# A sandwich layer on eight cores: the weight casts moved behind the first input loads, and a chunk's closing work moved into the next chunk's loop

## The reference, cut to what matters

```
def _L0_attn_ref(x, Wqkv, bqkv, Wout, bout):
    xc = x.reshape(N, Ls, Cc, Kk)                       # 32 blocks of 64
    qkv = jnp.einsum('nlck,cki->nlci', xc, Wqkv) + bqkv
    q, k, v = jnp.split(qkv, 3, axis=-1)
    scores = jnp.einsum('nlcd,nled->nldce', q, k) / Kk ** 0.5
    attn = jax.nn.softmax(scores, axis=-1)
    ctx = jnp.einsum('nldcm,nlcd->nldm', attn, v)
    ctx = ctx.transpose(0, 1, 3, 2)
    out = jnp.einsum('nlck,ko->nlco', ctx, Wout) + bout
    return out.reshape(N, Ls, Cc * Kk)

x = x + _layernorm(_L0_attn_ref(_layernorm(x), ...))
x = x + _layernorm((silu(xn @ w_gate.T) * (xn @ w_up.T)) @ w_down.T)   # xn = _layernorm(x)
```

## Time and profile before

| what | us |
|---|---|
| three runs | 6568.31, 6579.35, 6715.45 |
| median | 6579.35 |
| the profiled execution, whole time | 6572.25 |
| its span on the slowest core (core 3) | 6570.6 |
| spans of the other cores | 6551.8 to 6570.3 |
| busy on core 3: PE, DVE, ACT, POOL | 3205.5, 3231.0, 2051.9, 16.4 |

### The profile page before, as it was taken

One profiled execution on the slowest core, in us unless ns is written; L12 is line 12 of the kernel. 1 busy time (PEld: TensorE's weight loads), 2 busy tenths in 40 slices (PEclk: granted clock), 3 DMA queues, 4 the chain that ended last, 5 costly groups with the idle time before them and its releaser, 6 DMA issues.

```text
span 6570.6 us, 47652 instructions; the slowest of 8 cores (6551.8 to 6570.6 us)
## 1 busy us (share of the span) xinstructions
PE 3205.5 (49%) x15536; PEld 1485.4 (23%) x15536; DVE 3231.0 (49%) x3684; ACT 2051.9 (31%) x2953; POOL 16.4 (0%) x34
## 2 busy tenths in 40 slices
PE   0000010110048596850586867606767765089994
PEld 0000000000023233320232333203333322034441
DVE  0000008667757565747575657385756574721112
ACT  0000013444344444332443444324434433221210
POOL 0000000000000000000000000000000000000000
PEclk9999999655569797975797979757979887599997
DMA  9999970000023242321232322213323321144442
GB/s 113 111 111 110 111 81 0 7 7 0 7 74 122 64 136 80 112 65 38 86 116 71 122 93 100 65 38 100 103 87 106 103 87 64 35 144 141 154 141 87
DMA packets 177941, 556.83 MB, mean 85 GB/s; under 512 B 49568, under 2 KB 65952, under 8 KB 174496
## 3 DMA queue, kind: packets, MB, share of 16 engines
q1 hardware_dynamic: 171840, 442.60, 20.6%
q0 software_dynamic: 5856, 111.18, 15.0%
HBM read 639.73 MB, written 125.83 MB: 117 GB/s over the span
## 4 chain that ended last, share of the span: by engine, by line
DVE 30%; PE 24%; another core or an unknown queue 14%; ACT 12%; issue 12%; DMA 6%; DVEq 1%; ACTq 0%; SPq 0%
PE dps L415 10%; DVE es_sb L321 8%; DVE ctx_sb L330 6%; PE gps L353 6%; PE ups L363 6%; DVE zs_sb L752 4%; DVE zs_sb L746 4%; DMA wd_sb<-wdc 3%; ACT kd_sb L262 2%; DMA x2s_sb<-x2h 2%; ACT e_sb L376 1%; ACT m_sb L379 1%; ACT e_sb L373 1%; PE mps L189 1%
## 5 line engine op out<-in xcount | busy, mean ns | idle before, releaser
L353 PE MATMUL gps<-xn_sb,wg_sb 128*128 128x512 bf16 x4096 | 1002.9, 401 | 182.5 <-DVE gated_sb L388 167.5
L415 PE MATMUL dps<-gated_sb,wd_sb 128*128 128x512 bf16 x4096 | 920.1, 383 | 81.5 <-DMA wd_sb<-wdc 48.6
L363 PE MATMUL ups<-xn_sb,wu_sb 128*128 128x512 bf16 x4096 | 925.8, 379 | 0.0
L774 ACT ACTIVATE es_sb<-es_sb 128x4096 bf16<-128x4096 bf16 x256 | 922.0, 3602 | 11.4 <-DVE es_sb L737 11.4
L249 PE MATMUL mps<-xn_sb,wqkv_sb 128*128 128x128 bf16 x512 | 72.4, 302 | 1483.9 <-DVE xn_sb L804 1432.5
L763 ACT ACTIVATE rz_sb<-zf_sb 128x128 bf16<-128x128 bf16 x256 | 79.2, 309 | 2052.1 <-DVE zf_sb L756 2052.1
L202 DVE TENSOR_SCALAR st_sb<-mps 1x128 f32<-1x128 f32 x48 | 13.4, 279 | 1432.9 <-PE mps L189 1432.9
L383 DVE TENSOR_TENSOR t_sb<-m_sb,gps 128x512 bf16<-128x512 bf16 x256 | 175.9, 687 | 889.6 <-ACT m_sb L379 868.6
L321 DVE TENSOR_TENSOR es_sb<-es_sb,u_sb 128x4096 bf16<-128x4096 bf16 x256 | 586.7, 2292 | 27.7 <-DVE u_sb L312 1.4
L737 DVE TENSOR_TENSOR es_sb<-q_sb,kd_sb 128x4096 bf16<-128x4096 bf16 x256 | 586.0, 2290 | 24.4 <-DVE ctx_sb L330 0.9
L353 PEld LDWEIGHTS gps<-xn_sb,wg_sb 128*128 128x128 bf16 x4096 | 413.6, 102 | 741.4 <-issue 322.3
(11 more groups left out here) (85 smaller groups left out, 2033.0 us busy)
## 6 DMA issues: line engine op xcount, KB each, us to landing
wg_sb<-wgc SPq DMA_DIRECT2D x256, 512.0 KB, 3.5
wu_sb<-wuc SPq DMA_DIRECT2D x256, 512.0 KB, 3.3
wd_sb<-wdc SPq DMA_DIRECT2D x256, 512.0 KB, 3.4
wgc<-wgH POOLq DMA_DIRECT2D x4, 8192.0 KB, 434.4
wuc<-wuH POOLq DMA_DIRECT2D x4, 8192.0 KB, 509.6
wdc<-wdH POOLq DMA_DIRECT2D x4, 8192.0 KB, 585.3
yT<-outs_sb SPq DMA_DIRECT2D x64, 256.0 KB, 2.9
xb_sb<-xH POOLq DMA_DIRECT2D x16, 512.0 KB, 8.8
```

What stands on the lines that cost most here:

```text
L353: return tn.matmul(out=gps[pb].ap(), lhsT=wg_sb[pb].ap()[:, ft * 128:(ft + 1) * 128], rhs=xn2_sb.ap()[:, ft * W:(ft + 1) * W], start=(ft = ...
L363: return tn.matmul(out=ups[pb].ap(), lhsT=wu_sb[pb].ap()[:, ft * 128:(ft + 1) * 128], rhs=xn2_sb.ap()[:, ft * W:(ft + 1) * W], start=(ft = ...
L415: return tn.matmul(out=dps[pb].ap(), lhsT=wd_sb[wb].ap()[:, sh * 128:(sh + 1) * 128], rhs=gated_sb.ap()[:, ht * W:(ht + 1) * W], start=(ht ...
L774: ta = plan.op("A", lambda a, buf=buf: a.activation(out=buf.ap(), in_=buf.ap(), func=AF.Exp, scale=0.125), deps=[last[f"s_{c}_{j}"]], inc="A")
```

## The change

It has three parts. First, the casts are no longer issued ahead of everything: two are issued at the head of each pass of the loop until the list is empty, gate and up first, down last. Second, the closing work of a chunk is cut in two functions. `post_a` (the `wout` matmuls and the evictions to `ao_sb`) stays at the head of the next pass. `post_b` (all the rest, with `emit_xn2prep`, the spill and `dma_xb(c + 2)`) is called at j = 3 of the next chunk's attention loop, ahead of the pull. Third, there is no pull at j = 0, 1 and 2; at j = 3 there is a `pull(8)`, and from j = 4 on `pull(2)` as before. The number of atoms in a pass is the same. For c = -1 and c = 16, which have no attention, `post_a` and `post_b` follow each other directly.

```
-    for s in range(4):
-        for name_, dst_, src_ in (("g", wgc, wgT), ("u", wuc, wuT),
-                                  ("d", wdc, wdT)):
-            def fcache(g, dst_=dst_, src_=src_, s=s):
-                return g.dma_start(out=dst_[s * 2048:(s + 1) * 2048, :],
-                                   in_=src_[s * 2048:(s + 1) * 2048, :])
-            last[f"wc{name_}{s}"] = plan.op("G", fcache, inc=f"Dwc{name_}{s}")
+    _castd = {"g": (wgc, wgT), "u": (wuc, wuT), "d": (wdc, wdT)}
+
+    def emit_cast(name_, s):
+        dst_, src_ = _castd[name_]
+        def fcache(g, dst_=dst_, src_=src_, s=s):
+            return g.dma_start(out=dst_[s * 2048:(s + 1) * 2048, :],
+                               in_=src_[s * 2048:(s + 1) * 2048, :])
+        last[f"wc{name_}{s}"] = plan.op("G", fcache, inc=f"Dwc{name_}{s}")
+
+    CASTQ = [("g", 0), ("u", 0), ("g", 1), ("u", 1), ("g", 2), ("u", 2),
+             ("g", 3), ("u", 3), ("d", 0), ("d", 1), ("d", 2), ("d", 3)]
...
+        for _ in range(2):
+            if CASTQ:
+                emit_cast(*CASTQ.pop(0))
+
+        if 0 <= c < NC:
+            post_a()
+
         def pull(k):
...
-        if 0 <= c - 1 < NC:
-            cp = c - 1
-            ctx_tok = last[f"ctx_{cp}"]
...
+        def post_a():
+            if 0 <= c - 1 < NC:
+                cp = c - 1
+                ctx_tok = last[f"ctx_{cp}"]
...
+                last["ao"] = te
+                last[f"ctxdone_{cp}"] = te
+
+        def post_b():
+            if 0 <= c - 1 < NC:
+                cp = c - 1
+                tsq = plan.op("A", lambda a: a.activation(
+                    out=sq_sb.ap(), in_=ao_sb.ap(), func=AF.Square),
+                    deps=[last["ao"]] + dep("sq_free"), inc="A")
...
+            if 0 <= c - 1 < NC and (c - 1) % CPW == CPW - 1:
+                emit_xn2prep((c - 1) // CPW)
+
+            if 2 <= c + 2 < NC:
+                dma_xb(c + 2)
...
-                pull(2)
+                if j == 3:
+                    post_b()
+                if j >= 3:
+                    pull(8 if j == 3 else 2)
                 if j >= 1:
                     emit_uP(c, j - 1)
                 if j < NJ:
                     emit_exp(j)
+        else:
+            post_a()
+            post_b()
```

More of the change, by code:

```diff
@@ L615, in pull @@
                     emit_fin(a[1], a[2])
-        if 0 <= c - 1 < NC:
-            cp = c - 1
-            ctx_tok = last[f"ctx_{cp}"]
[L620 to L709, removed]
+        def post_a():
+            if 0 <= c - 1 < NC:
+                cp = c - 1
+                ctx_tok = last[f"ctx_{cp}"]
+                te = None
+                for grp in range(4):
+                    b = next_mbank()
+                    bank_dep = dep(f"pm{b}", "wout") + [ctx_tok]
+                    tk = None
+                    fst = True
+                    for i in range(4):
+                        mp = grp * 4 + i
+                        for par in (0, 1):
+                            m = 2 * mp + par
+                            def fn(tn, m=m, i=i, b=b, par=par):
+                                return tn.matmul(
+                                    out=mps[b].ap()[64 * par:64 * par + 64,
+                                                    i * T:(i + 1) * T],
+                                    lhsT=wout_sb.ap()[:, 64 * par:64 * par + 64],
+                                    rhs=ctx_sb.ap()[:, m * T:(m + 1) * T],
+                                    start=True, stop=True,
+                                    tile_position=(0, 64 * par),
+                                    skip_group_check=True)
+                            tk = plan.op("T", fn, deps=bank_dep if fst else (),
+                                         inc="T" if (i == 3 and par == 1) else None)
+                            fst = False
+                    def fe(a, grp=grp, b=b):
+                        return a.activation(
+                            out=ao_sb.ap()[:, grp * 4 * T:(grp + 1) * 4 * T],
+                            in_=mps[b].ap()[:, 0:4 * T], func=AF.Identity,
+                            bias=bo_sb.ap()[:, 0:1])
+                    d = [tk] + (dep("ao_free") if grp == 0 else [])
+                    te = plan.op("A", fe, deps=d, inc="A")
+                    last[f"pm{b}"] = te
+                last["ao"] = te
+                last[f"ctxdone_{cp}"] = te
```

49 lines of the change are left out of this document (added).

## The result

The changed kernel takes 6249.05 us as the median of ten runs (6127.99 to 6320.15), the kernel before in its own ten 6647.94 (6568.31 to 6790.34). The comparison gives a ratio of 0.9324, 95% interval 0.931 to 0.9339: faster by 6.8%. In both kernels some executions (five of ten before, six of ten after) are 2 to 3% longer, with a lower granted clock on the cores of one die, so the ratio and the times of runs from here on are of the others, 6128 to 6137 for the changed kernel.

What follows compares the result with a forecast made beforehand. The first 937 us were taken as bound by a queue order, input behind twelve casts. Sum: 6572.25 - 912 (front) + 68 (late load) + 4 (closing work) + 387 (piece of eight) = 6119, range 6035 to 6195.

Steps and rivals of the forecast that it cites:

- The front: Start of the kernel: with the casts behind the input, the first xb_sb lands at 25, not 936.8; gain 912.
- Chunk 2's late load: Chunk 1's first score product waits for chunk 2's input, queued behind two loads and four casts; cost 68.
- The third rival: Engines overlap the eight atoms at j = 3 as before, leaving only the queue's gain: 5732; chance 0.06.
- the fourth: Chunk 2's load is not held up because the DMA engines interleave it with the casts: 6051; chance 0.06.
- The closing work: Moved to j = 3, its waits come back there and it hides nothing: cost 4 over chunks 1 to 3.
- The boundary: Between chunks, L800 to first score product: falls to 30.3 from 47.3, or from 62.0 in chunks 4, 8, 12.
- The piece of eight: Eight atoms at j = 3, uncovered by attention, cost their full time: 129 a window, 387 over three windows.
- kind of chunk: Place in a four-chunk window; first to fifth score product: first 131.1, third 117.7, fourth 121.5; second: 78.6 to first down.
- the later loads have room: Input loads after chunk 2's land before they are wanted: chunk 3's near 491 for 572, chunk 4's near 646 for 805.
- the correction from the profiled execution to the median: Last step of the sum: profiled execution, 6572.25, is 0.1% under the median of three runs, so no correction.
- The first rival: Six casts from chunk 1 on starve beside DVE, delaying inputs of chunks 4, 5, 6 (+236, +309, +180): 6844; chance 0.04.
- The second rival: TensorE stays near its lower clock in the bursts, so 96 atoms take some 6.9 more each: 6782; chance 0.02.

Runs made afterwards that it cites:

- experiments 2 and 3: 2: changed kernel with pull(3) for pull(8) at j = 3, 5871 and 5877; 3: casts-only kernel plus the changed pulls alone, 5991 to 5998.
- casts-only kernel: Kernel before with only the first part of the change, casts in pairs at the head of each pass: 5809 to 5818, ratio 0.8813.
- experiment 4: Changed kernel with chunk 2's xb_sb load issued ahead of all casts: 6139 to 6169, ratio 0.9324.

## Why the prediction was right or wrong

**The front** held: 912 forecast, 912.6 measured. **Chunk 2's late load** held: 68 forecast, 67.1 waited, and chunk 1 is 67.5 longer. The third rival, that engines overlap the eight atoms, and the fourth, that the load is not held up, fall with these rows.

**The closing work.** The boundary is 28.7 to 29.7 in chunks 2 to 14 (30.3 forecast). That it "hides nothing" holds: chunk 3 came out at -0.3 (forecast +1.4), and chunks 1 and 2, less their waits, at +0.4 and +0.5.

**The piece of eight** held by kind of chunk: 132.4 for 131.1 in chunk 4, 120.8, 118.1 and 115.5 for 117.7 in the third chunks, 120.6, 119.9 and 122.1 for 121.5 in the fourth. In the second, where the forecast is of the first down, it starts 80.0 after the first score product in chunk 5, for 78.6. In all 374 for 387. The reason given, that the attention no longer covers the eight, was tested by experiments 2 and 3.

**The step that was left out** is the spill. The part on the late load said that "the later loads have room", and looked only at the loads on POOL's own queue; the transfers that SP issues while casts run were not priced. It cost 27.2 in the change, 87.1 in the casts-only kernel, and all the gain of experiment 4. The account's gain of 443 is within 10 of the forecast's 453 partly by luck: 27 more here stands against 13 less in chunks 4 to 15 and 5 less in small terms.

**The step that failed** is the last one of the sum, the correction from the profiled execution to the median, which was put at nothing: the profiled execution lies 0.1% under the median of three runs, "so I make no correction". In ten runs that term is not small. Those of the changed kernel fall into four at 6128 to 6137 and six at 6245 to 6320, and their median, 6249.05, is some 120 above the first group; in the kernel before it is 6647.94, 76 above the profiled 6572.25. So the median lies above my range of 6035 to 6195, while the ratio, 0.9324, is that of the forecast (6119 / 6572.25 = 0.931), and the first group is 0.1 to 0.3% above 6119. On which side of the range the median falls was decided by how many of ten executions came out long, which nothing in the prediction could tell; why they do stays open. Direction, size and mechanism were right, the absolute number was not: one of the three runs had already taken 6715, 2% more, and the top of the range should have been wider by as much.

**The first rival**, casts starved beside DVE, falls. DVE is busy 166 of the 250 us from 390 to 640 and 128 of 150 from 650 to 800, and the DMA engines move the same 111 and 112 GB/s, mean busy share 1.00 and 1.01 (110 and 1.00 in the kernel before, 100 to 900, with DVE idle). The two casts issued at 386 land at 567.1 and 642.3, 75.2 apart, where it was 75.95. All engines by stretch, core 0:

```profile
390.00:640.00 250.00, 19.81 (x162) 13.93 (x162) 165.78 (x168) 91.45 (x126) 0.00 (x0) 0.50 1.00 111
650.00:800.00 150.00, 0.00 (x0) 0.00 (x0) 127.98 (x123) 53.95 (x41) 0.00 (x0) 0.51 1.01 112
```

The rule of the Trainium skill cited there ("SBUF — State Buffer", "SBUF: two separate sides") does not show here: POOL's time for a cast is 0.55 to 0.62 us beside DVE's work and without it. Whether DVE's instructions here are of the two-port kind the rows don't tell. (The rival's price has a slip: the first of its three delays is 1037 - 805 = 232, not 236.) **The second rival**, a cold burst, falls too: the first 16 gate matmuls of chunk 6 take 5.78 in place of 3.62, the following ones 3.62. PE by stretch in the bursts of chunks 4 and 6, with the granted clock behind the busy time:

```profile
1131.00:1190.00 59.00, 56.15 (x247) 0.93 0.44 151
1833.00:1890.00 57.00, 55.01 (x245) 0.94 0.43 146
```

## What to carry to other kernels

When work is moved, look at every engine that it uses and ask what stands behind it in that engine's list. An engine that runs its list in order holds up all the rest when it meets eight atoms in a row, or a small matmul that waits for another engine. Before a large background transfer is put beside other work, look at each small transfer in its time, and at how many pieces it is cut into, not only at its bytes. And take a first gain apart before believing the whole: here one part gave 12% and the two others took 5% back.

## What the runs showed of the hardware that was not expected

Two queues on the same 16 DMA engines took turns by packet: 482 and 482 packets in the 100 us from 450 to 550, of 23 KB and of 256 bytes on average. A 512 KB transfer in 256-byte pieces took 257.9 us beside the casts, 335.3 and 370.9 where it started earlier, and 4.9 without them; in the three cases beside the casts it landed within 1 us of the last of them. In 4096-byte pieces it took 46.4. The Trainium skill, "DMA: Bandwidth & Descriptors", section "Queues, rings and completion order", says that each engine goes round robin between the queues that have work for it, a whole packet at a time. The trace agrees with that as far as the equal counts go: what the profile counts as a packet is one piece of 256 bytes in the one queue and one of 23 KB on average in the other, and in that stretch their turns came one for one.
